# Attention in a one-core layer kernel: the four uses of the last two PSUM banks are paired anew, and ScalarE's copies change places in a step

## The reference

```python
x = L0_attn_query                                 # (16, 256, 128)
xn = _layernorm(x)
# attention: 16 heads of 8 channels, causal mask
q, k, v = split(xn @ in_proj_weight.T)
a = softmax(q @ k.T / sqrt(8) + mask)
attn = (a @ v) @ out_proj_weight.T
# experts: one shared, 7 routed of which each token takes its best 2
#   expert(h) = (silu(h @ g.T) * (h @ u.T)) @ d, inner width 352
...
x = x + attn + ffn
```

## Time and profile before

| | before |
|---|---|
| median of 3 runs | 485.72 us (483.19 to 486.51) |
| profiled execution | span 485.8 us from the first to the last instruction; no time of its own beside the span is given |
| TensorE busy | 439.9 us (91%), 3983 matmuls |
| VectorE busy | 359.8 us (74%) |
| ScalarE busy | 312.8 us (64%) |
| GpSimd busy | 302.7 us (62%) |
| granted TensorE clock | 0.987 of full speed in the mean |

### The profile page before, as it was taken

One profiled execution on the slowest core, in us unless ns is written; L12 is line 12 of the kernel. 1 busy time (PEld: TensorE's weight loads), 2 busy tenths in 40 slices (PEclk: granted clock), 3 DMA queues, 4 the chain that ended last, 5 costly groups with the idle time before them and its releaser, 6 DMA issues.

```text
span 485.8 us, 12527 instructions
## 1 busy us (share of the span) xinstructions
PE 439.9 (91%) x3983; PEld 329.3 (68%) x3987; DVE 359.8 (74%) x804; ACT 312.8 (64%) x709; POOL 302.7 (62%) x439
## 2 busy tenths in 40 slices
PE   8888897988998989999889999998999899979995
PEld 4666565665666666666555688786877788868884
DVE  6885997987878877778774387585765777566987
ACT  2756676775867677767677676565565766555552
POOL 1326887997887888887888500755547487845300
PEclk9999999998999999999999999999999999989998
DMA  8776798999875555666356337787777767821762
GB/s 233 229 240 233 230 329 294 295 332 331 266 232 153 156 164 174 173 177 168 119 165 255 90 84 214 242 290 225 225 234 247 239 195 258 299 60 35 245 204 65
DMA packets 60415, 102.00 MB, mean 210 GB/s; under 512 B 11045, under 2 KB 29226, under 8 KB 59328
## 3 DMA queue, kind: packets, MB, share of 16 engines
q1 hardware_dynamic: 55872, 92.74, 61.2%
q0 software_dynamic: 4480, 8.47, 5.2%
HBM read 62.49 MB, written 39.46 MB: 210 GB/s over the span
## 4 chain that ended last, share of the span: by engine, by line
PE 62%; ACT 7%; POOL 6%; issue 5%; DVE 4%; SPq 4%; DMA 2%; another core or an unknown queue 2%; DVEq 0%; ACTq 0%; POOLq 0%
PE ps L850 11%; PE ps L848 11%; PE ps L849 11%; PE ps L917 6%; PE ps L978 6%; PE ps L925 4%; ACT sb_work L706 4%; POOL sb_work L620 3%; POOL xs L596 2%; PE ps L998 2%; DMA sb_ring<-qk 2%; PE ps L1143 2%; PE ps L981 2%; SPq L471 2%
## 5 line engine op out<-in xcount | busy, mean ns | idle before, releaser
L1343 DVE TENSOR_REDUCE sb_blockmax<-ps 128x6 f32<-128x768 f32 x128 | 121.5, 956 | 37.2 <-PE ps L925 32.4
L706 ACT ACTIVATE sb_work<-ps 128x768 f32<-128x768 f32 x128 | 104.7, 818 | 64.7 <-PE ps L913 63.5
L648 POOL DMA_INDIRECT ys<-sb_v_all,sb_xn_all x76 | 81.3, 1069 | 72.3 <-DVE sb_v_all L1464 52.6
L620 POOL TENSOR_SCALAR_AFFINE_SELECT sb_work<-sb_work 128x512 f32<-128x512 f32 x128 | 82.2, 646 | 27.6 <-ACT sb_work L706 25.5
L849 PE MATMUL ps<-sb_ring,sb_wb 128*128 128x512 f32 (+1 forms) x231 | 83.6, 362 | 0.0
L1443 DVE TENSOR_TENSOR sb_v_all<-ps,sb_v_all 128x512 f32<-128x512 f32 (+1 forms) x93 | 57.5, 618 | 24.4 <-ACT sb_v_all L796 10.6
L596 POOL DMA_INDIRECT xs<-sb_xn_all,sb_posu x64 | 62.9, 983 | 10.6 <-issue 10.6
L917 PE MATMUL ps<-sb_ring 32*128 32x256 f32 x256 | 49.5, 377 | 20.7 <-ACT sb_work L706 10.1
L796 ACT ACTIVATE sb_v_all<-ps 128x512 f32<-128x512 f32 (+1 forms) x93 | 49.7, 534 | 10.5 <-PE ps L850 5.4
L917 PEld LDWEIGHTS ps<-sb_ring 32*128 32x128 f32 x256 | 25.6, 183 | 44.9 <-issue 38.4
L848 PE MATMUL ps<-sb_ring,sb_wb 128*128 128x512 f32 (+1 forms) x138 | 51.6, 374 | 3.3 <-issue 1.8
(11 more groups left out here) (168 smaller groups left out, 1089.0 us busy)
## 6 DMA issues: line engine op xcount, KB each, us to landing
sb_wb<-wd SPq DMA_DIRECT2D x75, 384.0 KB
sb_ring<-qk SPq DMA_DIRECT2D x64, 256.0 KB
wd<-sb_wb SPq DMA_DIRECT2D x8, 1152.0 KB, 5.9
xs<-sb_o_all SPq DMA_DIRECT2D x19, 260.0 KB, 4.2
qk<-sb_ring SPq DMA_DIRECT2D x32, 128.0 KB
sb_work<-ys SPq DMA_DIRECT2D x16, 256.0 KB, 3.2
sb_xn_all<-xs SPq DMA_DIRECT2D x15, 260.0 KB
sb_o_all<-w SPq DMA_DIRECT2D x8, 384.0 KB, 3.9
```

The costliest lines, as they stand in the source:

```text
L620: pool.affine_select(out=o, in_=o, compare_op=ALU.is_ge, fill=0.0, base=0, pattern=[[0, 4], [1, 128]], channel_multiplier=-1)\
L648: pool.indirect_dma_start(out=ys_d, out_offset=bass.IndirectOffsetOnAxis(ap=row, axis=0), in_=yst[i % NYS][:, EMB * j:EMB * j + EMB], in_o ...
L706: act.activation(part.rearrange("p (k h q) -> p h k q", h=2, q=128), ps[:, 4:6, 0:HEAD].rearrange("p h (k q) -> p h k q", q=128), ACT.Exp, ...
L1343: dve.tensor_reduce(blockmax[:, a:b + 1, 0:3], ps[:, a:b + 1, 0:HEAD].rearrange("p h (k c) -> p h k c", c=128), AX.X, ALU.max).then_inc(s[ ...
```

## The change

The sums (L979, L982) move from bank J to bank X, columns 0 to 255, beside the side work, and the transposes (L998) from bank X to bank J, columns 256 to 511, beside the queries' maxima. The waits move with them:

- the transposes wait for the queries' copy (`q4b`) and no more for the side work's readers; the sums wait for these readers (`bank_read`) and for the sums' copy before (`OT`), and no more for `q4b`;
- `maxima` waits for the copy of the transposed sums (`xc`), and side work for the sums' copy (`OT`) of the same step in place of `xc`.

On ScalarE the sums' copy moves from behind the second exponential to before it, behind `unscaled`, without the wait for `Mt`; in the step after the last quad it keeps its place. The values' copy moves from the end of steps j = 0 to steps j = 2 of the sequence before, in front of the queries' copy (sequence 0: step 0).

```diff
             def unscaled(n):
...
-                view = X[:, 0:256].rearrange("p (t h c) -> p t h c", t=2, c=32)
+                view = J[:, 256:512].rearrange("p (t h c) -> p t h c", t=2, c=32)
                 act.activation(xo[c % 2][:, :, j, :, :], view[:, :, :, 0:HD + 1], ACT.Copy).then_inc(s["xc"], 1)
+            def summed(n):
+                act.wait_ge(s["PV"], n + 1)
+                if isq(n - 1):
+                    act.wait_ge(s["T"], n)
+                act.activation(ot[:, :], X[:, 0:256], ACT.Copy).then_inc(s["OT"], 1)
+            def own_values(b):
+                act.wait_ge(s["lg"], b + 1)
...
             def step(n):                         # ScalarE
...
                         if k and isq(n - 2):
                             unscaled(n - 2)
+                        if k and isq(n - 1):
+                            summed(n - 1)
...
-                if isq(n - 1):
-                    act.wait_ge(s["PV"], n)
-                    if isq(n + 2):
-                        act.wait_ge(s["Mt"], n + 3)
-                    if isq(n - 2):
-                        act.wait_ge(s["T"], n - 1)
-                    act.activation(ot[:, :], J[:, 256:512], ACT.Copy).then_inc(s["OT"], 1)
+                if isq(n - 1) and not isq(n):
+                    summed(n - 1)
+                if n >= 0 and j == 2 and isb(b + 1):
+                    own_values(b + 1)
                 if n >= 0:
                     queries(n + 2)
-                if j == 0 and isb(b):
...
+                if n == 0:
+                    own_values(0)
...
             def maxima(m):                       # TensorE
...
+                if isq(m - 4):
+                    pe.wait_ge(s["xc"], m - 3)
...
             def sums(n):
-                if isq(n + 2):
-                    pe.wait_ge(s["q4b"], n + 3)
+                bank_read(n)
+                if n:
+                    pe.wait_ge(s["OT"], n)
...
-                    pe.matmul(J[32 * h:32 * h + 32, 256:512], v_sb[b % 2][:, 0, 4 * j + h, :],
+                    pe.matmul(X[32 * h:32 * h + 32, 0:256], v_sb[b % 2][:, 0, 4 * j + h, :],
...
             def step(n):
...
-                    bank_read(n - 1)
                     pe.wait_ge(s["OT"], n - 1)
+                    if isq(n + 1):
+                        pe.wait_ge(s["q4b"], n + 2)
...
-                        last = pe.transpose(X[:, 128 * t:128 * t + 128], ot[:, 128 * t:128 * t + 128], ident)
+                        last = pe.transpose(J[:, 256 + 128 * t:384 + 128 * t], ot[:, 128 * t:128 * t + 128], ident)
...
-                if isq(n - 2) and has_side(n):
-                    pe.wait_ge(s["xc"], n - 1)
+                if isq(n - 1) and has_side(n):
+                    pe.wait_ge(s["OT"], n)
                 side(n)
...
-                    pe.wait_ge(s["OT"], NQ)      # experts' stage, u == 4
+                    pe.wait_ge(s["xc"], NQ)
...
-                    pe.wait_ge(s["xc"], NQ)      # experts' stage, u == 5
+                    pe.wait_ge(s["OT"], NQ)
```

More of the change, by code:

```diff
@@ L690, in unscaled @@
                     act.wait_ge(s["nm"], c - 1)
-                view = X[:, 0:256].rearrange("p (t h c) -> p t h c", t=2, c=32)
+                view = J[:, 256:512].rearrange("p (t h c) -> p t h c", t=2, c=32)
                 act.activation(xo[c % 2][:, :, j, :, :], view[:, :, :, 0:HD + 1], ACT.Copy).then_inc(s["xc"], 1)
+            def summed(n):
[5 more added lines that the diff above has]
+                act.wait_ge(s["lg"], b + 1)
+                act.wait_ge(s["v1"], 2)
+                if b >= 2:
+                    act.wait_ge(s["PV"], 4 * (b - 1))
+                act.activation(v_sb[b % 2][:, :, :, 0:HD],
+                               v_all[:, 2 * b:2 * b + 2, :].rearrange("p s (h d) -> p s h d", h=HEADS), ACT.Copy)\
+                    .then_inc(s["va"], 1)
             def step(n):
@@ L977, in sums @@
                 for h in range(4):
-                    pe.matmul(J[32 * h:32 * h + 32, 256:512], v_sb[b % 2][:, 0, 4 * j + h, :],
+                    pe.matmul(X[32 * h:32 * h + 32, 0:256], v_sb[b % 2][:, 0, 4 * j + h, :],
                               p[:, h // 2, h % 2, 1:3, :], start=True, stop=False, skip_group_check=True)
                 for h in range(4):
-                    last = pe.matmul(J[32 * h:32 * h + 32, 384:512], v_sb[b % 2][:, 1, 4 * j + h, :],
+                    last = pe.matmul(X[32 * h:32 * h + 32, 128:256], v_sb[b % 2][:, 1, 4 * j + h, :],
                                      p[:, h // 2, h % 2, 0, :], start=False, stop=True,
```

## The result

| | before | changed |
|---|---|---|
| median of 9 runs | 485.72 us (480.09 to 491.57) | 488.14 us (486.63 to 492.16) |
| ratio, changed to before | | 1.0086, 95% interval 1.0053 to 1.0118 |
| profiled span | 485.8 us | 488.0 us |
| opening of step 24, of step 63 | 132.16, 267.33 | 130.90, 269.12 |
| first halves, steps 24 to 62, summed | 71.7 us | 68.3 us |

A forecast was written before the change was run, and what follows sets the result against it. It took attention as a chain of short hand-overs, first halves set by TensorE, second by the exponential. Terms -3.3 + 2.0 + 0.5 = -0.8 us against 485.8 gave 485.0 us, range 480.5 to 491.

The forecast's parts named there:

- the term of the sums' copy: ScalarE, between the two exponentials: the copy leaves the second exponential 0.06 us spare, so price 0.
- the first rival: Second halves: the moved copy holds the second exponential 0.14 us, 63 times, +8.8 us, giving 493.8 us; chance 0.14.
- My own sign of being wrong: New profile, second halves: a second exponential starting past 0.52 us after the opening would mean slower.
- First halves: First halves after side work: transposes stop waiting for VectorE and the sums wait instead; sum -3.3 us.
- my list for the whole phase: Attention steps after side work: savings of 0.6, 0.7 and 2.0 us, sum -3.3 us.
- The side wait: Second halves: side work waits for the sums' copy, 0.08 us in each of 25 halves, +2.0 us, bounds 0 and 4.3.
- my third rival: Side work starts cold after its wait, 0.19 us more in each of 25 halves: +4.8 us, 489.8 us; chance 0.11.
- The values' copy: ScalarE: the copy moves from the head of j = 1 steps to j = 2 and stays hidden; price 0.
- the tail: After the last quad: only which copy a wait names changes, and both are done by then; price 0.
- What swallows gains: Query and key loads up to step 20, GpSimd's sends from step 23: gains and costs come out smaller than the sum.

The follow-up runs named there:

- e13: Kernel before with GpSimd's 64 sends put off until attention has ended, 485.7 us batch; steps 24 to 63 take 127.1 us.
- e14: Changed kernel with GpSimd's 64 sends put off until attention has ended, 485.7 us batch; steps 24 to 63 take 124.3 us.
- e11: Kernel before with only the sums' copy moved between the exponentials, old banks; ratio 1.0052 to the kernel before, in a 485.7 us batch.
- e5: The changed kernel run again without any edit; ratio 1.0011 to the kernel before, in a 467.3 us batch.
- e3: Kernel before with only the values' copy moved to steps j = 2; ratio 0.9987 to the kernel before, in a 467.0 us batch.
- e1: Kernel before with only the sums' copy moved between the exponentials, old banks; ratio 0.9999 to the kernel before, in a 467.0 us batch.
- e2: Changed kernel, sums' copy back behind the second exponential in steps without side work, values' copy behind queries' copy; ratio 1.0019 to the kernel before.
- e6: Kernel before with only the sums' copy moved between the exponentials, old banks, as e1; ratio 0.9980 to the kernel before, 467.3 us batch.
- e4: Changed kernel with GpSimd's 64 sends put off until attention has ended, 467.0 us batch; steps 24 to 63 take 124.3 us.

## Why the prediction was wrong

**The step that failed** is the term of the sums' copy: "0.06 spare. ... Price 0". The cover of 0.06 us was read in steps 12 and 13, where no rows are sent, and taken for all 63 steps. In the stretch with sends the sums are announced 0.25 to 0.8 us after the second half opens, the copy waits for that, and the exponential starts 0.28 behind it. Second halves of steps 24 to 62 grew by 6.4 us, 0.16 a half, beside the 0.14 of the first rival (+8.8 over 63 steps). The rival had the right mechanism, and it was half luck that its size fits: its 0.14 came from a copy that starts on time and an exponential that starts afresh behind it. I looked for the danger in how ScalarE spaces its instructions, and that spacing came out as read (0.28). It is the start of the copy that was off. I gave the case 0.14. My own sign of being wrong, a second exponential past 0.52, came true.

**The trace of before held the sign.** Its second exponentials start 0.49 to 0.52 after the opening up to step 23, but for one (step 18), and 0.66 in the mean from 24 on. Step 43 is such a half: the scores end at 200.98 + 0.22 = 201.20 by the model, ScalarE has been idle for 1.22 us, and the exponential starts at 201.49.

```profile
93.78 0.22 PE L913 MATMUL ps<-sb_ring 32*128 32x128 f32 x2
...
200.98 0.22 PE L913 MATMUL ps<-sb_ring 32*128 32x128 f32 x2
```

```profile
201.49 0.81 ACT L706 ACTIVATE sb_work<-ps 128x768 f32<-128x768 f32 x1 [1.22 <-PE ps L913]
```

0.29 between the end of the producer and the start of an idle consumer, where step 13 has 0.05 (L913 ends at 94.00, the exponential starts at 94.05), is an end announced later than modelled: the other things that the exponential waits for are done long before, and the trace has the update of its semaphore at 201.46. I priced the new wait by modelled ends all the same.

**First halves** came out at the places that I named and near the size, but not for one reason. Transposes start 0.6 after the opening, step 13's half is 1.72 (I had worked out 1.83), and from 24 to 62 first halves gave back 3.4 us, against 3.3 in my list for the whole phase. The queries' copy, which I thought would hold the transposes by 0.1, does so by 0.05 (weight loads at 0.55 in step 13 and in the j = 1 steps from 25 to 49, against 0.50 in a plain step). With the sends taken out the places are clean: the 14 first halves after side work (steps 25 to 50) take 27.2 us in e13 and 24.1 in e14, all others together 43.0 and 42.9.

I had put all of this down to the new pairing of the banks. e11, whose banks are paired as before, contradicts that: its first halves of steps 24 to 62 take 68.6 us, 3.1 less than the kernel before, where I had expected it to gain nothing. In step 13 its first half takes 1.85, between 1.99 and 1.72:

```profile
88.26 0.38 PE L913 MATMUL ps<-sb_ring 32*128 32x256 f32 x2
...
90.11 0.38 PE L913 MATMUL ps<-sb_ring 32*128 32x256 f32 x2
```

So a good part of the gain comes with the copy's move or with the longer second halves, and no run has the new pairing with the copy left behind in every step. How much the pairing is worth alone is not shown.

**The side wait** was put at 0.08 a half, 2.0 us. It costs 0.02 where the sums end on time (1.48 against 1.46 in step 13 and in e5's step 36). Where they are late it costs 0.12 in step 36 (1.72 against e11's 1.60), and 0.8 us over the 14 halves with projections from step 24 on, about 0.06 a half. The cold start of the side work, my third rival, is not seen: with the sums on time it starts 0.61 after the opening, 0.09 late and no more.

**The values' copy and the tail** at 0 stand (e3; the tail has no experiment of its own).

**What swallows gains** was half of it. In the batches without the lag the stretch takes 131.0 to 131.9 in e1, e2, e3, e5 and e6, whatever is changed, and 124.3 without the sends (e4). Between 130 and 260 us TensorE's sums wait 14 times for GpSimd's masks in e5, 4.7 us in all, and once, 0.4 us, in e14. So GpSimd's pace sets the stretch there, and the 2.7 us that the change is worth without sends don't show.

**Left open:** why TensorE's sums are announced late while GpSimd issues indirect DMAs in one kind of batch and not in the other, and whether the matmuls themselves end late or only the semaphore's update comes late. Nothing that I edited tells these apart. Also open is the exact split of the 3.0 us between the copy (e11: 137.8 - 135.2 = 2.6) and the side wait (the rest), since a stretch varies by more than 0.4 between executions. No version beat the kernel before beyond its interval; e6's 0.9980 includes 1, and e11 is slower.

## What to carry to other kernels

A wait that is put in front of the instruction that ends last needs cover in every stretch, not in the one with the best view: look at an idle consumer's start against its producer's modelled end in each stretch, and take the difference as the true lateness. Moving a wait to where the slack is 0.06 us trades a small gain for a loss that other work, and even another batch of runs, can switch on. When a kernel takes 467 us in one batch and 485 in another, compare only within a batch, and repeat the decisive experiment where the effect shows. And when several edits go in together, give each predicted gain a run of its own: the run made to isolate the loss (e11) was the one that showed that the gain had been put down to the wrong edit in part.

## What the runs showed of the hardware

The late announcement of TensorE's sums goes with GpSimd's indirect DMAs and with the kind of batch. On the 485 us kind the copy that waits for the sums starts 0.31 us after their modelled end in step 36 and up to 0.79 after it in step 47. In e5, and in steps before 24, it starts 0.07 after it, and with the sends taken out, in a batch of the 485 us kind, it is 0.07 again (e14). The sends themselves take the same time in both kinds, 0.98 us each. The granted clock doesn't explain it: it was 1.00 between 160 and 215 us in the kernel before.

The traces of the two kinds differ in one more thing. On the 485 us kind they lack many records of semaphore updates: of the 128 of the exponential they hold 104 in the changed kernel and 107 in the kernel before, and 125 in e5. With the sends taken out every exponential has its record (e13, e14). Whether this belongs with the late updates is not shown.
